# A graph network's layer on one core: TensorE's products grouped by kind, and a head in which TensorE picks the table's rows

## The reference

```python
h = jnp.maximum(_layernorm(x, axis=-1), 0.0)
# objects = h, relations = edge_attr_128, senders = src, receivers = dst
rel_inputs = jnp.concatenate([objects[senders], objects[receivers], relations], axis=-1)
rel_effects = _mlp(rel_inputs, re_w1, re_b1, re_w2, re_b2)      # 384 -> 256 -> 128
agg_effects = jax.ops.segment_sum(rel_effects, receivers, num_segments=objects.shape[0])
effect_inputs = jnp.concatenate([objects, agg_effects], axis=-1)
updated_objects = _mlp(effect_inputs, ea_w1, ea_b1, ea_w2, ea_b2)  # 256 -> 256 -> 128
return x + updated_objects
```

## Time and profile before

| | |
|---|---|
| median of 3 runs | 987.33 us (987.01 to 987.4) |
| the profiled execution | 985.56 us, its span 983.8 us |
| granted TensorE clock, mean | 0.990 |
| busy: PE, DVE, ACT, POOL | 932.3, 737.0, 549.7, 582.1 us |
| first product of the first joint step | 80.74 us |
| first product of the first pair step | 940.14 us |

### The profile page before, as it was taken

How to read it: one execution, slowest core, us unless ns; L and a number is a source line. 1 busy time by engine, 2 the same in 40 slices (tenths; PEclk the granted TensorE clock), 3 DMA queues, 4 the chain that set the end, 5 groups by cost and what they waited for, 6 DMA issues and landing times.

```text
span 983.8 us, 19952 instructions
## 1 busy us (share of the span) xinstructions
PE 932.3 (95%) x5994; PEld 827.9 (84%) x5994; DVE 737.0 (75%) x2051; ACT 549.7 (56%) x1083; POOL 582.1 (59%) x609
## 2 busy tenths in 40 slices
PE   1577999999999999999999999999999999999997
PEld 1456888889889888988988988888988988898876
DVE  3665878778777778878877887877887777887652
ACT  1134566556566556656656656656656655665653
POOL 6883566566567566566566656656656656655121
PEclk9978999999999999999999999999999999999999
DMA  4324454454454454454444445445445445434331
GB/s 135 98 78 121 136 160 128 135 164 135 128 165 141 123 166 143 122 163 138 134 148 151 136 140 157 131 139 161 132 130 165 140 125 166 142 121 151 92 108 55
DMA packets 114340, 132.90 MB, mean 135 GB/s; under 512 B 18084, under 2 KB 70250, under 8 KB 114224
## 3 DMA queue, kind: packets, MB, share of 16 engines
q1 hardware_dynamic: 101440, 105.43, 34.7%
q0 software_dynamic: 12784, 26.10, 9.3%
HBM read 92.46 MB, written 39.00 MB: 134 GB/s over the span
## 4 chain that ended last, share of the span: by engine, by line
PE 91%; POOL 4%; DVE 2%; issue 1%; ACT 1%; SPq 0%; DMA 0%; POOLq 0%; DVEq 0%
PE l_ps L502 32%; PE l_ps L520 26%; PE l_ps L510 16%; PE agg_ps L474 9%; PE edge_ps L458 4%; PE node_ps L466 4%; POOL gath L364 2%; POOL picked_i L406 0%; DVE st L715 0%; POOL lo L385 0%; DMA dst_all<-in_dst_cols 0%; DMA win<-rel_rows 0%; ACT hid L623 0%; DVE res L787 0%; SPq L270 0%
## 5 line engine op out<-in xcount | busy, mean ns | idle before, releaser
L380 POOL TENSOR_TENSOR xb<-xin,b2n 128x512 f32<-128x512 f32 x98 | 126.7, 1293 | 256.9 <-DVE res L787 256.9
L364 POOL DMA_INDIRECT gath<-in_x,src_all x196 | 191.8, 979 | 55.8 <-issue 50.2
L364 POOL DMA_INDIRECT gath<-in_x,dst_all x196 | 186.0, 949 | 61.4 <-issue 61.4
L623 ACT ACTIVATE hid<-l_ps,b1e 128x512 f32<-128x512 f32 x98 | 67.3, 687 | 226.6 <-PE l_ps L510 226.6
L623 ACT ACTIVATE hid<-l_ps,b1n 128x512 f32<-128x512 f32 x196 | 134.6, 688 | 103.8 <-PE l_ps L510 103.7
L520 PE MATMUL l_ps<-w2n,hid 128*128 128x128 f32 x1568 | 191.0, 275 | 0.8 <-ACT hid L623 0.8
L520 PEld LDWEIGHTS l_ps<-w2n,hid 128*128 128x128 f32 x1568 | 186.5, 192 | 5.7 <-ACT hid L623 1.2
L753 DVE TENSOR_SCALAR h<-gath,rs,shift 128x128 f32<-128x128 f32 x392 | 177.2, 520 | 1.8
L502 PE MATMUL l_ps<-hi,w1n_hi 128*128 128x512 f32 x392 | 167.2, 427 | 1.5 <-ACT hid L623 1.5
L630 ACT ACTIVATE h<-xin,shift,rs 128x128 f32<-128x128 f32 x392 | 160.3, 482 | 0.1
L502 PE MATMUL l_ps<-hi,w1n_lo 128*128 128x512 f32 x392 | 154.8, 395 | 0.0
(11 more groups left out here) (78 smaller groups left out, 1293.1 us busy)
## 6 DMA issues: line engine op xcount, KB each, us to landing
win<-rel_rows SPq DMA_DIRECT2D x392, 66.0 KB
xin<-in_x_tiles SPq DMA_DIRECT2D x98, 256.0 KB, 4.4
out<-res SPq DMA_DIRECT2D x98, 256.0 KB, 2.0
rel_rows<-rel_row SPq DMA_DIRECT2D x49, 264.0 KB, 2.2
ea_in<-in_ea_t SPq DMA_DIRECT2D x49, 256.0 KB, 4.3
gath<-in_x,src_all POOLq DMA_INDIRECT x196, 2.5
gath<-in_x,dst_all POOLq DMA_INDIRECT x196, 2.6
w1e<-in_L_gnn_re_w SPq DMA_DIRECT2D x1, 384.0 KB, 3.5
```

Of the source, the lines that this page charges most:

```text
L364: nc.gpsimd.indirect_dma_start(gath[b][:, s, k, :], None, x, bass.IndirectOffsetOnAxis(ap=idx[:, e * T + k:e * T + k + 1], axis=0)).then_i ...
L380: nc.gpsimd.tensor_tensor(xb[r][:, :, :], xin[r][j % 2][:, :, :], b2[1][:, :].unsqueeze(1).to_broadcast([P, T, D]), ALU.add).then_inc(xb_s ...
L623: nc.scalar.activation(hid[r][:, c, :], l1_ps[c][:, :], ACT.Relu, bias=b[:, c:c + 1]).then_inc(hid_set, 1)
```

## The change

1. Joint step of PE: all of layer 1 (edges, node 1, node 2), then turn and window of the next node 1, the turn of the next edges, layer 2 of the edges and of node 1, turn and window of the next node 2, layer 2 of node 2. Node 2's turn and window so belong to the pair before, and the first pair's stand in `enter`. The pair steps likewise.
2. ACT, DVE, POOL and the DMA queue (SP) are put in an order to match: ACT splits `normalise` between the hidden layers; DVE does the statistics first, then `node_results(2)`, `invert`, all of `normalise_edges`, both marks; SP loads both windows first; POOL does half of a gather, `low_ea`, `keep_x(2)`, the other half.
3. The parts of the edge attributes get two buffers of their own (`ea_hi`, `ea_lo`); in the head DVE makes the low part, not POOL.
4. The constants come before `gather(0)` on POOL, and the receivers' rows are loaded before the first edge attributes.
5. The rows of the table are picked by PE: `in_this` marks the row that holds a bound, and five products with it select that row of `drow` (197 columns each). The counting, the row numbers and the five indirect DMAs go, and `decide` and both weight splits stand ahead of group 0's statistics.
6. The branch stands before the third edge step, and SP loads the first windows there, ahead of the third group's store.
7. In the head's edge step `layer2` stands before the next `turn_edges`, and DVE's `edge_results(e)` before `invert` and `normalise_edges(e + 1)`.

```diff
         def run(eng, edge_step, enter, joint_step, pair_step):
-            for e in range(FIRST):
-                edge_step(e, e == FIRST - 1, True)
+            for e in range(FIRST - 1):
+                edge_step(e, False, True)
             eng.wait_ge(ctrl_set, 1)
             fits = eng.snap(eng.value_load(ctrl[0:1, 0:1], min_val=0, max_val=1))
             with eng.If(fits > 0):
+                edge_step(FIRST - 1, True, True)
                 enter(True)
...
@@ SP
             def joint_step(e, j):
-                if j + 1 < NJ:
-                    load_window(1, j + 1)
+                for r in (1, 2):
+                    if j + 1 < NJ:
+                        load_window(r, j + 1)
+                if e + 2 < EG:
+                    load_ea(e + 2)
                 if j > 0:
                     store(2, j - 1, True)
...
@@ POOL
+            pool.wait_ge(consts, 6)
+            nc.gpsimd.affine_select(out=ident[:, :], in_=ident[:, :], compare_op=ALU.not_equal, fill=1.0,
+                                    base=0, pattern=[[-1, P]], channel_multiplier=1).then_inc(consts, 1)
+            pool.wait_ge(idx_loaded, 32)
+            gather(0)
...
-            gather(1)
-            pool.wait_ge(row_no_set, 1)
-            for q in range(5):
-                nc.gpsimd.indirect_dma_start(picked_i[:, q, :], None, dst_rows,
-                                             bass.IndirectOffsetOnAxis(ap=row_no[:, q:q + 1], axis=0)).then_inc(rows_picked, 16)
...
             def joint_step(e, j):
                 set_dst(e)
+                if e + 2 < EG:
+                    gather(e + 2, range(0, 2))
+                if e + 1 < EG:
+                    low_ea(e + 1)
                 if j > 0:
                     keep_x(2, j, True)
                 if e + 2 < EG:
-                    gather(e + 2)
-                if e + 1 < EG:
-                    low_ea(e + 1)
+                    gather(e + 2, range(2, T))
                 if j + 1 < NJ:
                     keep_x(1, j + 1, True)
...
@@ PE
             for q in range(5):
-                last = nc.tensor.matmul(agg_ps[0:NT, q:q + 1], before_row[:, bass.ds(q, NT, 4)], ones[:, :], start=True, stop=True)
-            last.then_inc(counted, 1)
+                last = nc.tensor.matmul(picked(q), in_this[:, bass.ds(q, NT, 4)], drow[:, 0:RUN + 1], start=True, stop=True)
+            last.then_inc(rows_picked, 1)
...
             def joint_step(e, j):
                 turn = edge_turn(e, True)
-                layer1(0, e, turn, 0)
-                layer1(0, e, turn, 1)
-                turn_nodes(2, j)
-                sum_window(2, j)
-                layer1(1, j, turn + 1, 0)
-                layer1(1, j, turn + 1, 1)
-                layer2(0, turn)
-                layer1(2, j, turn + 2, 0)
-                layer2(1, turn + 1)
-                if e + 1 < EG:
-                    turn_edges(e + 1)
-                layer1(2, j, turn + 2, 1)
+                for r, n in ((0, e), (1, j), (2, j)):
+                    for c in range(C):
+                        layer1(r, n, turn + r, c)
                 if j + 1 < NJ:
                     turn_nodes(1, j + 1)
                     sum_window(1, j + 1)
+                if e + 1 < EG:
+                    turn_edges(e + 1)
+                layer2(0, turn)
+                layer2(1, turn + 1)
+                if j + 1 < NJ:
+                    turn_nodes(2, j + 1)
+                    sum_window(2, j + 1)
                 layer2(2, turn + 2)
...
@@ ACT, joint step after the change
+                if e + 1 < EG:
+                    high_ea(e + 1, True)
                 hidden(0, turn, 0, before_edge(e, True))
+                if more:
+                    deviations(e + 1, slice(0 if e + 1 < EG else 2 * T, ST))
                 hidden(0, turn, 1, before_edge(e, True))
...
+                    normalise(1, j + 1, True, range(0, 1))
                 hidden(1, turn + 1, 0, before_node(1, j, True))
...
+                    normalise(1, j + 1, True, range(1, 3))
                 hidden(1, turn + 1, 1, before_node(1, j, True))
...
@@ DVE
             compare_rows()
             split_weights(0)
-            statistics(0, 0, None)
-            pick_rows()
...
+            low_ea(0)
+            find_starts()
+            decide()
...
+            split_weights(1)
+            prepare(0, 0, None)
             normalise_edges(0, range(T))
             low_edges(0)
```

More of the change, by code:

```diff
@@ L311, in edge_step @@
                     load_ea(e + 2)
+                if last and fast:
+                    load_window(1, 0)
+                    load_window(2, 0)
                 store_rel(e, fast)
             def enter(fast):
[L315 to L319, removed]
+                if not fast:
                     load_windows(1, 0)
@@ L590, in pair_step @@
                     add(1, j + 1)
+                layer2(1, turn)
+                if j + 1 < NJ:
+                    turn_nodes(2, j + 1)
+                    add(2, j + 1)
                 layer2(2, turn + 1)
@@ L673, in joint_step @@
                 hidden(1, turn + 1, 1, before_node(1, j, True))
-                if j + 1 < NJ:
-                    normalise(1, j + 1, True)
+                if more:
+                    normalise(1, j + 1, True, range(3, T))
                 hidden(2, turn + 2, 0, before_node(2, j, True))
-                if j + 1 < NJ:
-                    normalise(2, j + 1, True)
+                hidden(2, turn + 2, 1, before_node(2, j, True))
+                if more:
+                    high_nodes(1, j + 1, True)
@@ L880, in edge_step @@
                 if e + 1 < EG:
-                    prepare(e + 1, e + 1, 0 if last else None)
-                    normalise_edges(e + 1, range(T))
-                if e == 0:
-                    find_starts()
+                    what = (e + 1, e + 1, 0 if last else None)
+                    if e + 1 < FIRST:
+                        low_ea(e + 1)
+                    statistics(*what)
+                    totals(*what)
+                    squares(*what)
+                    spreads(*what)
@@ L898, in enter @@
-                low_features(1, 0)
-                low_sums(1, 0)
+                for r in (1, 2):
+                    (mark if fast else mark_all)(r, 0)
+                    low_nodes(r, 0)
             def joint_step(e, j):
+                more = j + 1 < NJ
                 what = (e + 1, some(e + 1, EG), some(j + 1, NJ))
+                statistics(*what)
+                totals(*what)
+                squares(*what)
+                spreads(*what)
                 if j > 0:
                     node_results(2, j - 1, True)
-                statistics(*what)
@@ L906, in joint_step @@
-                totals(*what)
-                low_features(2, j)
-                squares(*what)
-                low_sums(2, j)
-                spreads(*what)
-                mark(1, j + 1)
                 invert(*what)
                 if e + 1 < EG:
-                    normalise_edges(e + 1, range(0, 2))
-                edge_results(e, True)
-                if e + 1 < EG:
-                    normalise_edges(e + 1, range(2, T))
-                mark(2, j + 1)
-                node_results(1, j, True)
+                    normalise_edges(e + 1, range(T))
@@ L920, in joint_step @@
+                for r in (1, 2):
+                    if more:
+                        mark(r, j + 1)
+                if more:
+                    low_nodes(1, j + 1)
                 if e + 1 < EG:
                     low_edges(e + 1)
-                low_features(1, j + 1)
-                low_sums(1, j + 1)
+                edge_results(e, True)
+                node_results(1, j, True)
+                if more:
+                    low_nodes(2, j + 1)
             def pair_step(j, fast):
+                more = j + 1 < NJ
```

267 lines of the change are left out of this document (123 added, 144 removed).

## The result

The changed kernel takes 1026.18 us (median of 4 runs, 1025.8 to 1026.85); the kernel before took 987.17 us on the same chip (4 runs, 985.52 to 987.4). The ratio is 1.040, 95% interval 1.0382 to 1.0418: 4% slower, where 975 us and a gain of 1.2% were forecast.

The account below looks back on a forecast made before the run. PE's gapless products were taken to bound the joint steps, leaving gains in head and tail. Span 72.0 + (859.4 - 0.7) + 40.7 = 971.4 us, 12.4 less than 983.8; 987.33 - 12.4 gives 975 us, range 968 to 985.

Parts of the forecast that it names:

- The head: Stretch before the joint steps: group 0 normalised at 22.3, first joint product at 72 us instead of 80.74.
- the joint steps: Main stretch, 859.4 us with PE always busy: no new waits of PE, only 0.7 us saved.
- the pair steps: Tail after the joint steps: two steps of 13.3 and a last of 14.1, together 40.7 us, 3.0 less.
- One place is tight: Joint step: `shift` meets POOL's `low_ea`, is done at 5.85 instead of 4.65; PE does not wait, 0.1 us to spare.
- second rival: Joint step: `shift` gets no turn between `low_ea` and `keep_x(2)`; PE waits 1.3 a step, 60 us, 1035; chance 0.08.
- if not: Reading of the skill's blocking rule where DVE is not let in between two POOL operations; leads to the second rival.
- Short waits in each step: Rival in the joint steps: PE waits 0.1 to 0.3 in each of 46, 5 to 14 us, 980 to 989; chance 0.15.
- The order of the products: PE's joint steps: three fewer switches of kind a step, at 0.005 each, save 0.7 us (0 to 2.8).
- half-clock rival: Head stays at half clock: 15.5 a group, first joint product at 80 to 82, some 983 to 985; chance 0.12.
- The other bound: Head: first joint product at 69 us if PE runs at full clock throughout.
- The constant: Amount by which the median time lies over the profiled span: 3.5 us.

Follow-up runs that it names:

- experiment 1: Changed kernel with POOL's whole gather first in the joint step, then `low_ea` and `keep_x(2)`: 966.38 us, 0.979 of the kernel before.
- experiment 2: Changed kernel with only `keep_x(2)` moved, behind the gather's second half; `low_ea` stays between the halves: 971.8 us, 0.985 of the kernel before.
- experiment 3: Changed kernel, nothing moved, with one more wait on POOL: `keep_x(2)` starts only when `low_ea` is written: 972.37 us, 0.985 of the kernel before.
- experiment 5: Changed kernel with a third POOL operation, a repeated `keep_x(2)` addition nobody reads, between `low_ea` and `keep_x(2)`: 1096.65 us, 1.112 of the kernel before.
- experiment 9: Kernel of experiment 1 with an early ACT square root and the first pair's two `keep_x` behind the fifth group's gather: 966.1 us, 0.978.
- experiment 7: Kernel of experiment 1 with an unused 32-byte tile that puts the operands 32 bytes off a multiple of 64: 979.84 us, 0.993 of the kernel before.
- experiment 10: Kernel of experiment 1 with the early square root and the first pair's two `keep_x` right behind `low_ea(3)`, ahead of the fifth group's gather: 964.4 us, 0.978.

## Why the prediction was wrong

By its own sum the span was to be 971.4 and was 1024.3, 52.9 more. The head has 5.0 of it (77.03 instead of 72.0), the joint steps 48.3 (906.97 instead of 858.7), the pair steps -0.4 (40.3 instead of 40.7).

**The step that failed** is "One place is tight", where I took `shift` as done at 5.85: held by `low_ea` and let in before `keep_x(2)`. The timing that led there was right to 0.1: `low_ea` began at 4.32 of the step (4.4 forecast), `shift` at 4.49 (4.45), `keep_x(2)` at 5.57 (5.6). But `shift` ended at 6.92. What then follows is the second rival as it was written: 1.3 us a step, 60 in all; measured 58.3. It gives 1035 where 1026 was measured, mainly since the products had become cheaper (below). Experiments 1, 2, 3 and 5 show the hold from four sides (0.17, 1.2, 1.2 and 3.6 us of `shift` for no operation, one, two with a gap, and three without).

The evidence for the wrong choice was a single pair of rows, the cast at 33.66 and POOL's copy at 34.45. It showed that DVE can come in between two POOL operations, not that it does so between these two. Before that copy POOL executes waits that are already met, and the copy is another kind of operation. The first can't be the difference: `keep_x(2)` too stands behind waits that are met (for its x and for the result of the tile before), and it let nothing in. A copy stands behind the second `keep_x` in experiment 9 as well, begun at 65.70, and there the hold ended at 65.85, while the copy took its usual 0.20. No run varied the kind of operation, so that it is the kind stays open. Experiment 3 shows that a wait for a result not yet written is enough.

The same trace had rows for the other side, which I overlooked. Two normalisations of DVE, 0.34 each when alone, began at 31.17 and 31.43 and ended at 33.21 and 33.27, past three clearings of POOL that stand back to back:

```profile
31.17 2.10 DVE L753 TENSOR_SCALAR h<-gath,rs,shift 128x128 f32<-128x128 f32 x2
...
31.94 0.23 POOL L408 MEMSET end_row<- 128x132 f32 x1
32.09 1.04 POOL L410 MEMSET rel_row<- 128x528 f32 x2
33.18 0.13 POOL L412 MEMSET end_row<- 128x1 f32 x1
```

The third ended at 33.12; the fourth stands behind a wait for POOL's own clearings, and in that gap DVE was let go, as in experiment 3. Nor did the trace show the simple hold only once: in 41 joint steps a normalisation was held to the end of `low_ea` and took 1.90 instead of 0.34, for instance that from 429.77 to 431.67. With these rows, 0.08 for a mechanism of 60 us was far too little, and the range left it out.

The Trainium skill, "SBUF — State Buffer", section "Who interferes with whom", has the second to issue blocked for the whole of the first. The 1.20 us in experiment 3 agree with it; of a third instruction behind the first it says nothing, and there 2.43 and 3.63 us were measured. The prediction had this case as "if not", and chose against it.

**Short waits in each step** (0.15) did not come: with one hold, in experiments 2 and 3, the median step is 18.50, and PE waited 0.5 in two steps of each. In the changed kernel a PE wait came in 43 steps, but it is the hold's.

**The order of the products** was priced at 0.7 saved. The sum took 0.005 for a switch of kind where its own reading gave 0.01, which would make 1.4. With the operands where they were it costs about 0.02 a step, 1 us (experiment 7 against before); with them at a multiple of 64 it gains 0.08, some 4 us. The term that was missing is the place: 18.705 - 18.45 = 0.26 a step, 12 us in the new order. With the hold and without this gain the changed kernel would have come out near 1038, by this estimate. That 1026 is the nearer to the forecast is luck.

**The head.** Group 0's normalisation came at 24.69 instead of 22.3. The first two of these rows carry that, DVE's wait for the weights and ACT's table load; the other two belong to the third group:

```profile
10.18 0.56 DVE L820 CAST w1e_hi<-w1e 128x768 fp32r<-128x768 f32 x1 [4.00 <-DMA b2e<-in_L_gnn_re_b]
...
22.62 1.28 ACT L592 ACT_TABLE_LOAD   x1 [16.35 <-DVE spread L739]
...
48.75 2.51 DVE L746 SCALAR_TENSOR_TENSOR shift<-total,rs 128x8 f32<-128x8 f32 x1
...
48.75 2.47 POOL L381 TENSOR_TENSOR xb<-xin,b2n 128x512 f32<-128x512 f32 x2
```

I had the comparison done and then the split of the weights, but not that these land only at 10.2; and I had not asked where the first square root stands. An early one brought the normalisation to 23.23 (experiment 9). The periods were 12.9, 13.7 and 13.6 instead of 13.4, 13.0 and 11.8: the second has the hold behind both `keep_x`, 2.5 and not 0.8, the same mistake; in the third PE was granted 0.74, after a stretch without an instruction from 47.90 to 52.00. This is part of the half-clock rival (0.12), which asked for 80 to 82 and got 77.0. The other bound, 69 at full clock, doesn't follow from the prediction's own terms: 22.3 and four times 11.3 make 67.5. The entry took 12.1 instead of 11.3, at 0.67. `low_ea(0)` on DVE at 11.65 and no wait of the first two masks for their windows came as forecast.

**The pair steps** were right: 984.00, 997.31, 1010.63, so 13.3 each. The constant was off by 1.6: the median lies 1.9 over the profiled span now, not 3.5, for the profiled execution of the kernel before was itself 1.8 below the median.

## What to carry to other kernels

Before an operation is moved on POOL, look at what DVE does in that place and in the half microsecond ahead of it, and at what stands right behind it on POOL: in these kernels `shift`, with two inputs in SBUF, and the normalisations, with one, paid for the whole back-to-back group, and when another engine's work hangs on such an operation that price is paid in every step. Separate the group (experiment 2 did it with gathers, experiment 3 with a wait for POOL's own result), or move it to where DVE makes statistics, as in experiment 10, or reads PSUM; in the kernel before, eight statistics took 1.64 and two low parts from PSUM 1.29 beside a `keep_x`, as they did without one. When one row of a trace speaks for a cheap case and the price of the other is five times the gain, the range has to hold it; and when tiles are added, look at where the streamed operands come to stand.

## What was unexpected of the hardware

- DVE's 16-element `shift` stayed held over two and three consecutive POOL operations (2.43 and 3.63 us), and was let in (1.20 us) when POOL waited for its own result between them, which cost POOL 0.13 us.
- The hold can begin before POOL's operation is shown to begin: `shift`, started 0.6 us ahead of `low_ea` within a gather, took 3.18 us instead of 0.17.
- With 32 bytes more ahead of the moving operands (and of the tiles behind them), 512-column products start 0.233 us apart instead of 0.227 or the other way round: 7 us of the kernel before, 13 us of the kernel in experiment 1.
- With a wait of PE of 2.2 us in every step the granted clock fell in about every fourth (0.87 over 11.6 us), at 1.6 us each; with waits of 1.0 us it stayed at 1.00.
